# Another order for the sixteen-tile round of an attention kernel: scores and keys-as-rows in runs of two pairs, value products in runs of two

## The chip, the cores and the metric

The kernel runs on one core of a Trainium2 chip. The metric is the device time of one execution in microseconds. Engines are called as in the profile: PE is TensorE (matmuls; PEld its weight loads), DVE VectorE, ACT ScalarE, POOL GpSimd, SP SyncE, which issues the DMAs.

## The reference

Four sequences (B = 4) of 2048 rows of 256 numbers go through two layers, each with a residual and a layer norm.

```python
# first layer: 16 heads of 16; the value row is weighed with the sum of the row's softmax over m
att = softmax(einsum('blhd,bmhd->blmh', q, k) * scale, axis=2)
opt = einsum('blmh,blhd->blhd', att, v)
x = layernorm(x + opt @ w_out.T + b_out)
# second layer: the 4 best of 16 heads of 64 are chosen for each sequence, then attention
idx = sort(top_k(softmax(mean(x @ Wr + br, axis=1)), 4))
score = softmax(einsum('bhqd,bhkd->bhqk', Qs, Ks) * scale, axis=-1)
x = layernorm(x + (score @ Vs) @ Wo + bo)
```

All inputs and outputs are float32.

## The kernel before

A program on the host, `plan()`, writes out the order of the work of each engine before the kernel is built, and the kernel issues its instructions in these orders. For PE it keeps seven lists of units, each in order of due times, which `work_lists()` makes. Whenever PE is free in the planner's own small model of time, it takes the unit with the earliest due time among the heads of the lists whose inputs are ready and for which banks of PSUM are free. A unit that can't start yet is passed over for one of another list.

The units that matter here, with their lines:

- **A**, a tile of the first layer: two matmuls (L987) give 128 x 1024 scores of one head in two banks, DVE takes the negated row maximum (`nmax`, L1320), ACT the exponential with its sum (L1131, an ACTIVATE and a read of the accumulator). The banks are free when ACT is done. A batch has 16 heads x 16 row tiles x 2 halves = 512 tiles.
- **S**, a score of the second layer: four matmuls (L1052) for two heads at once, in the two halves of the array's rows, into two banks. DVE reduces them to maxima (`smax`, L1386), which frees the banks.
- **T**, the keys-as-rows form of the same product: four matmuls (L1067) and two small ones that subtract the maximum (L1070), in two banks. ACT takes the exponential into one of six slots of `probs` (L1246), which frees the banks.
- **V**, a value product: four matmuls (L1087) in the two halves of the array's columns. Four steps accumulate in one bank, from the first to ACT's copy of it (L1256). V of a step needs the exponentials of all four steps.
- POOL sums the exponentials (L896). Once in 16 steps a group ends: M (L1058) turns the maxima to rows, D (L1102) sums over partitions, R (L1110) spreads the reciprocals, and FQ, FO, FK, FV (L960, L945) are projections.

PSUM has eight banks; A, S and T take two each. While batch b is in its second layer, the tiles of batch b + 1 run between its steps. This is laid down in rounds of four steps (`BURST = 4`): a string gives the due times of a round's units by their place in it. A round takes S of steps ahead and T and V of steps one group (16 steps) behind. `ROUNDS[16]` has 16 tiles, `ROUNDS[12]` has 12, `ROUNDS[0]` (last batch) none, and `LEAD` opens the first and the last batch. Which is used:

```python
        if r < behind or b == B - 1 and k < behind:
            spots = LEAD
        elif b + 1 < B:
            spots = ROUNDS[16 if A_TILES - given[b] > 12 * (rounds - k) - EARLY else 12]
        else:
            spots = ROUNDS[0]
```

with 32 rounds in a batch, `behind` = 4, `given` the tiles already given out (32 at a batch's start, `AHEAD`), and `EARLY` = 8.

Of the kernel before, what the change touches and what calls it, by code (L numbers as in the profile page):

```python
# [42 lines left out]
BURSTS = STEPS // BURST  # L43
AHEAD = 32
EARLY = 8
ROUNDS = {0: "TSSTSTSTVVVV", 12: "AASTAASTSATASTAAAVVAAVAV", 16: "STAASTAASTAASTAAAVAVAAVAAVAA"}
LEAD = "SAAAASAAAASAAAASAAAATTTTVVVV"


# [28 lines left out]
def work_lists():  # L78
# [37 lines left out]
    for r in range(B * rounds + behind):  # L116
# [3 lines left out]
# [4 lines that stand above are left out]
        take = {"S": r * BURST, "T": r * BURST - STEPS, "V": r * BURST - STEPS}  # L124
# [1334 lines left out]
```

## Time and profile before

| | us |
|---|---|
| median of three runs | 3801.54 |
| lowest and highest | 3799.16, 4034.18 |
| the profiled execution | 3804.1 |
| its span, first to last instruction | 3802.2 |
| PE busy | 3517.9 |
| DVE busy | 3359.8 |
| ACT busy | 3063.9 |
| POOL busy | 1795.5 |

Busy times are of the whole span. Matmuls overlap in PE's pipeline, so a busy PE is not a PE at its peak. Idle time of an engine counts only where the others wait for it. The mean granted clock of TensorE is 0.953 of full speed (2.4 GHz).

### The profile page before, as it was taken

Reading aid. Unit: us, or ns where it says so; the run is one execution under the profiler, and the core shown is the slowest. Engines: PE = TensorE matmul, PEld = TensorE weight load, DVE = VectorE, ACT = ScalarE, POOL = GpSimd, SP = SyncE. Lnnn points to the kernel's source line nnn. Section 1 sums busy time; section 2 is a strip of 40 time slices with the busy share of each in tenths; the row PEclk is TensorE's granted clock in tenths of the full one; section 3 lists DMA queues with packets and bytes.
Section 4 is the critical chain, followed back from the end, with each engine's and each line's share of the span. In section 5 each row is a group of like instructions: output and inputs, shape, how many; then the busy total and the mean of one; then the engine's idle time right before and its main releaser. Section 6 shows DMA issues by size and latency. Waiting matters only on the chain.

```text
span 3802.2 us, 42635 instructions
## 1 busy us (share of the span) xinstructions
PE 3517.9 (93%) x14196; PEld 1270.9 (33%) x14196; DVE 3359.8 (88%) x3347; ACT 3063.9 (81%) x5097; POOL 1795.5 (47%) x1296
## 2 busy tenths in 40 slices
PE   8999989889999999899999999899999999899998
PEld 4323323332232323333232323433232323343333
DVE  7999999989999999889999999889999998567776
ACT  6999999879989998788999898788999998423333
POOL 6134433404443545445344445544444445657776
PEclk9988888889999999999999999899999999899999
DMA  6122222200010101200010101200010100100000
GB/s 201 50 81 81 86 76 66 85 17 17 17 28 17 28 17 37 77 13 24 17 28 17 28 17 31 82 9 29 17 28 17 28 17 17 49 1 12 12 12 12
DMA packets 117198, 142.67 MB, mean 38 GB/s; under 512 B 33395, under 2 KB 100467, under 8 KB 116979
## 3 DMA queue, kind: packets, MB, share of 16 engines
q1 hardware_dynamic: 116978, 139.95, 12.5%
q8 instruction: 114, 1.87, 0.2%
q14 instruction: 106, 0.86, 0.1%
HBM read 89.55 MB, written 50.33 MB: 37 GB/s over the span
## 4 chain that ended last, share of the span: by engine, by line
PE 44%; DVE 31%; ACT 17%; issue 4%; POOL 2%; SPq 1%; DMA 0%; DVEq 0%; POOLq 0%; ACTq 0%
DVE nmax L1320 21%; ACT ps L1131 15%; PE ps L1087 10%; PE ps L987 9%; PE ps L1052 7%; DVE smax L1386 7%; PE ps L1067 6%; PE ps L960 5%; PE ps L945 3%; PE ps L1102 1%; PE ps L1070 1%; DVE y L786 1%; DVE st L1298 1%; POOL y L786 1%; DVE y L1295 1%
## 5 line engine op out<-in xcount | busy, mean ns | idle before, releaser
L1320 DVE TENSOR_REDUCE nmax<-ps 128x1 f32<-128x1024 f32 x2048 | 2383.7, 1215 | 154.8 <-PE ps L987 146.3
L1131 ACT ACTIVATE ps<-ps,nmax 128x1024 f32<-128x1024 f32 x2048 | 2236.3, 1109 | 274.3 <-DVE nmax L1320 245.9
L987 PE MATMUL ps<-stack 96*128 96x512 bf16 x4524 | 1341.1, 402 | 174.2 <-ACT ps L1131 90.5
L896 POOL TENSOR_TENSOR facc<-facc,probs 128x1024 f32<-128x1024 f32 x443 | 1043.6, 2356 | 680.3 <-ACT probs L1246 603.1
L987 PEld LDWEIGHTS ps<-stack 96*128 96x128 bf16 x4524 | 326.7, 100 | 1314.0 <-ACT ps L1131 806.9
L1386 DVE TENSOR_REDUCE smax<-ps 128x2 f32<-128x1024 f32 x512 | 620.0, 1217 | 129.0 <-PE ps L1052 128.3
L1052 PE MATMUL ps<-fk,fq 64*128 64x512 f32 x2048 | 576.3, 645 | 29.6 <-ACT ps L1131 27.6
L1067 PE MATMUL ps<-fq,fk 64*128 64x512 f32 x2048 | 549.2, 615 | 5.3 <-DVE probs L1416 2.6
L1087 PE MATMUL ps<-probs,vals 128*64 128x512 f32 x2048 | 519.6, 614 | 5.4 <-DVE oT L1434 3.6
L1131 ACT ACTIVATION_READ_ACCUMULATOR ps<-ps,nmax 128x1 f32 x2048 | 451.9, 221 | 0.0
L1246 ACT ACTIVATE probs<-ps 128x1024 f32<-128x1024 f32 x384 | 391.5, 1020 | 70.1 <-PE ps L1070 69.8
L1235 ACT ACTIVATE probs<-probs 128x1024 f32<-128x1024 f32 x128 | 135.2, 1056 | 206.9 <-DVE probs L1416 146.0
L1067 PEld LDWEIGHTS ps<-fq,fk 64*128 64x128 f32 x2048 | 188.2, 189 | 266.1 <-issue 126.8
L1052 PEld LDWEIGHTS ps<-fk,fq 64*128 64x128 f32 x2048 | 165.3, 188 | 273.4 <-ACT ps L1131 156.4
L902 POOL TENSOR_TENSOR oacc<-oacc,part 128x512 f32<-128x512 f32 x72 | 90.9, 1263 | 275.8 <-ACT part L1256 275.8
L1087 PEld LDWEIGHTS ps<-probs,vals 128*64 128x64 f32 x2048 | 117.2, 136 | 277.6 <-issue 213.6
L762 POOL CAST fk<-vals 128x512 bf16<-128x512 f32 x60 | 36.6, 610 | 355.9 <-DVE vals L1326 331.9
L893 POOL TENSOR_TENSOR facc<-probs 128x1024 f32<-128x1024 f32 x32 | 75.3, 2355 | 262.5 <-ACT probs L1246 228.9
L1416 DVE TENSOR_TENSOR probs<-ps,stack 128x1024 f32<-128x1024 f32 x128 | 154.7, 1216 | 42.9 <-PE ps L1067 23.5
L1070 PE MATMUL ps<-frows,minus 64*128 64x512 bf16 x768 | 150.0, 383 | 0.0
L960 PE MATMUL ps<-fq,w_inT 128*128 128x512 f32 x256 | 141.4, 674 | 1.1 <-DVE qk_bias L1279 0.3
L960 PE MATMUL ps<-x1T,wqk_sel 128*128 128x512 f32 x256 | 133.8, 621 | 4.4 <-DMA bqk_sel<-in_L_ffn_bq 4.2
(134 smaller groups left out, 2021.0 us busy)
## 6 DMA issues: line engine op xcount, KB each, us to landing
stack<-qk_levels SPq DMA_DIRECT2D x768, 64.0 KB, 2.2
qk_levels<-fk SPq DMA_DIRECT2D x64, 384.0 KB, 2.5
probs<-in_L_attn_x SPq DMA_DIRECT2D x16, 512.0 KB, 3.9
v_rows<-vals SPq DMA_DIRECT2D x16, 512.0 KB, 2.7
vrows<-v_rows SPq DMA_DIRECT2D x16, 512.0 KB, 3.4
res<-in_L_attn_x SPq DMA_DIRECT2D x16, 512.0 KB, 4.0
x_rows<-y SPq DMA_DIRECT2D x16, 512.0 KB, 2.9
res<-x_rows SPq DMA_DIRECT2D x16, 512.0 KB, 3.9
```

What stands on the lines that cost most here:

```text
L896: pool.tensor_tensor(total, total, probs[:, slot, :], ALU.add).then_inc(facc_ready, 1)
L960: last = pe.matmul(bank(banks[0]), wT(cc), columns(cc), start=(cc == 0), stop=(cc == KC - 1))
L987: last = pe.matmul(bank(banks[i]), stack[0:SK, hd % 2, 0, t * P:(t + 1) * P], stack[0:SK, hd % 2, 1, col:col + CH], start=True, stop=True)
L1052: last = pe.matmul(bank(banks[h]), fq[rows, pair, qs:qs + P], fk[rows, pair, ks:ks + CH], start=True, stop=True)
L1067: last = pe.matmul(bank(banks[h]), fk[rows, pair, s * P:(s + 1) * P], fq[rows, pair, c * CH:(c + 1) * CH], start=True, stop=b + 1 == B)
L1070: last = pe.matmul(bank(banks[h]), minus16[rows, :], frows[rows, g % 2, :], start=False, stop=True)
L1087: last = pe.matmul(ps[rows, into, :], vals[:, s, (2 * pair + h) * FD:(2 * pair + h + 1) * FD], probs[:, slot_of(b, g, s), h * CH:(h + 1) * ...
L1131: act.activation(src, src, ACT.Exp, bias=nmax[:, b % 2, half, t, hd:hd + 1], scale=-1.0, accum_out=esum[:, b % 2, half, t, hd:hd + 1]).the ...
L1246: act.activation(probs[:, slot_of(b, g, s), :].rearrange("p (h n) -> p h n", h=2), two_banks(banks), ACT.Exp, scale=float(FD) ** -0.5).the ...
L1320: dve.tensor_reduce(nmax[:, b % 2, half, t, hd:hd + 1], two_banks(banks), AX.XY, ALU.min).then_inc(min_ready, 1)
L1386: dve.tensor_reduce(smax[:, g % 2, s // NCH, :, s % NCH], two_banks(banks), AX.X, ALU.max).then_inc(smax_ready, 1)
L1416: dve.tensor_tensor(probs[:, slot_of(b, g, s), :].rearrange("p (h n) -> p h n", h=2), two_banks(banks), bc[:, g % 2, :].rearrange("p (h n) ...
```

## The change

One string of due times gets another order. It has the same 28 units: four S, four T, four V and sixteen A. Before, each pair S T had two tiles behind it (three behind the last), and V came singly with one or two tiles between. After, two pairs S T S T run together, then four tiles, again two pairs and four tiles, then two V, four tiles, two V, four tiles.

```diff
@@ -43,7 +43,7 @@
 BURSTS = STEPS // BURST
 AHEAD = 32
 EARLY = 8
-ROUNDS = {0: "TSSTSTSTVVVV", 12: "AASTAASTSATASTAAAVVAAVAV", 16: "STAASTAASTAASTAAAVAVAAVAAVAA"}
+ROUNDS = {0: "TSSTSTSTVVVV", 12: "AASTAASTSATASTAAAVVAAVAV", 16: "STSTAAAASTSTAAAAVVAAAAVVAAAA"}
 LEAD = "SAAAASAAAASAAAASAAAATTTTVVVV"
```

No instruction is added or taken away. The orders of all engines, and the banks that the units get, come out of the planner anew.

## Rows read from the trace of the kernel before

**Rows 1.** The page, busy time and share of the span by engine.

```profile
PE 3517.9 (93%) x14196; PEld 1270.9 (33%) x14196; DVE 3359.8 (88%) x3347; ACT 3063.9 (81%) x5097; POOL 1795.5 (47%) x1296
```

**Rows 2.** Groups by line from 1700 to 2200 us: shapes, count, busy, mean, idle before.

```profile
L1386 DVE TENSOR_REDUCE smax<-ps 128x2 f32<-128x1024 f32 x80 | 97.3, 1216 | 4.7 <-PE ps L1052 4.7
```

**Rows 3.** Waits of DVE from 1700 to 2200 us: total us, times, longest.

```profile
DVE nmax L1320 <- PE ps L987: 20.1, 55, 1.5
DVE smax L1386 <- PE ps L1052: 4.7, 10, 0.9
```

**Rows 4.** DVE's timeline of one round: start, us, instruction, idle before and its cause.

```profile
1964.18 1.22 DVE L1386 TENSOR_REDUCE smax<-ps 128x2 f32<-128x1024 f32 x1
...
1975.57 3.48 DVE L1320 TENSOR_REDUCE nmax<-ps 128x1 f32<-128x1024 f32 x3
1979.23 1.22 DVE L1320 TENSOR_REDUCE nmax<-ps 128x1 f32<-128x1024 f32 x1 [0.20 <-PE ps L987]
1980.78 6.88 DVE L1320 TENSOR_REDUCE nmax<-ps 128x1 f32<-128x1024 f32 x6 [0.32 <-PE ps L987]
1987.58 1.21 DVE L1386 TENSOR_REDUCE smax<-ps 128x2 f32<-128x1024 f32 x1
```

**Rows 5.** Windows of 10 us: length, busy PE, PEld, DVE, ACT, POOL, clock, DMA.

```profile
1680.00:1690.00 10.00, 10.00 (x47) 4.42 (x47) 8.45 (x8) 8.68 (x15) 5.71 (x3) 1.00 0.01 2
...
1810.00:1820.00 10.00, 10.00 (x34) 3.67 (x34) 6.58 (x8) 7.00 (x13) 0.61 (x1) 0.67 0.31 81
```

**Rows 6.** PE's timeline of the same round.

```profile
1965.35 0.60 PE L987 MATMUL ps<-stack 96*128 96x512 bf16 x2 [0.31 <-ACT probs L1246]
1965.88 1.13 PE L1052 MATMUL ps<-fk,fq 64*128 64x512 f32 x4
1966.84 1.02 PE L1067 MATMUL ps<-fq,fk 64*128 64x512 f32 x4
...
1968.02 0.60 PE L987 MATMUL ps<-stack 96*128 96x512 bf16 x2
...
1976.72 1.94 PE L1087 MATMUL ps<-probs,vals 128*64 128x512 f32 x8
1978.59 0.60 PE L987 MATMUL ps<-stack 96*128 96x512 bf16 x2
1979.13 1.08 PE L1087 MATMUL ps<-probs,vals 128*64 128x512 f32 x4
1980.14 1.04 PE L987 MATMUL ps<-stack 96*128 96x512 bf16 x4
1981.11 1.08 PE L1087 MATMUL ps<-probs,vals 128*64 128x512 f32 x4
...
1983.30 1.17 PE L987 MATMUL ps<-stack 96*128 96x512 bf16 x4 [0.58 <-ACT ps L1131]
...
1985.98 1.13 PE L1052 MATMUL ps<-fk,fq 64*128 64x512 f32 x4 [0.49 <-ACT ps L1131]
```

**Rows 7.** PE's timeline elsewhere, S and T without tiles between.

```profile
1507.01 1.02 PE L1067 MATMUL ps<-fq,fk 64*128 64x512 f32 x4
...
1508.08 1.02 PE L1052 MATMUL ps<-fk,fq 64*128 64x512 f32 x4
1508.94 1.02 PE L1067 MATMUL ps<-fq,fk 64*128 64x512 f32 x4
```

**Rows 8.** ACT's timeline, the exponential that follows 1980.78 on DVE.

```profile
1982.04 1.09 ACT L1131 ACTIVATE ps<-ps,nmax 128x1024 f32<-128x1024 f32 x1 [0.34 <-DVE nmax L1320]
```

**Rows 9.** PE's timeline in batch 0, the first and last of five single tiles.

```profile
562.31 0.60 PE L987 MATMUL ps<-stack 96*128 96x512 bf16 x2
...
566.51 0.60 PE L987 MATMUL ps<-stack 96*128 96x512 bf16 x2 [0.49 <-ACT ps L1131]
```

**Rows 10.** Windows of 1 us there, columns as in the windows above.

```profile
567.00:568.00 1.00, 0.51 (x2) 0.13 (x2) 1.00 (x2) 1.00 (x3) 0.00 (x0) 0.70 0.00 0
568.00:569.00 1.00, 0.94 (x3) 0.13 (x2) 1.00 (x2) 1.00 (x3) 0.00 (x0) 0.50 0.42 127
```

## The prediction

> **What bounds the kernel now.** I read the page's busy times first: PE stands at 93% and DVE at 88% of the span [rows 1], so either could be the bound, and the average doesn't decide it. So I went to the stretch that the change touches. The sixteen-tile round is used 74 times: batch 0 enters its fifth round with 96 of 512 tiles given out, and the rule in the code then picks it 22 times; batches 1 and 2 begin with 32 given and pick it 26 times each. From 1700 to 2200 us (inside batch 1) there are 80 score reductions [rows 2], four to a round, so 20 rounds in 500 us: **25 us a round**. One microsecond a round is 74 us, 1.95% of the time; about 2% is also what a measurement of this kernel can tell from no change.
>
> In that stretch DVE waits for PE for 20.1 us ahead of tile minima and 4.7 us ahead of score maxima [rows 3], 1.24 us a round. That is all that any new order can win from DVE: 92 us over the 74 rounds.
>
> Then one undisturbed round in the timeline. On DVE [rows 4] it runs from the score at 1964.18 to the score at 1987.58, 23.4 us for 20 reductions. Six in a row begin at 1980.78 and the next at 1987.58, so one takes 1.13 us from start to start and 20 take 22.7. The 0.7 us left over are two gaps in the part with value products: three reductions begin at 1975.57, so the fourth could begin at 1978.96 but begins at 1979.23 (0.27 late); the next could begin at 1980.36 and begins at 1980.78 (0.42). In the part with scores and keys-as-rows DVE has no gap. There PE is the one that waits, and for banks. So in most rounds **the loop DVE, ACT, free bank, PE is the bound, with DVE full**, and PE's own time is cover. Some rounds are otherwise: at 1680 to 1690 us PE is busy all of the time and DVE 8.45 of 10 [rows 5]; the two batches' first four rounds carry late projections and look like this, 8 rounds in all.
>
> **The change, part by part.**
>
> *Fewer turns on PE.* From a tile to a score PE needs 0.53 us (1965.35 to 1965.88), score to keys-as-rows 0.96, keys-as-rows to the next tile 1.18 (1966.84 to 1968.02) [rows 6]. A tile ahead of another tile costs 0.43: a tile, a tile and the turn to a value product take 0.97 (1980.14 to 1981.11), and one tile with that turn 0.54 (1978.59 to 1979.13) [rows 6]. In a run without tiles, keys-as-rows to score takes 1.07 and score to keys-as-rows 0.86 [rows 7]. Two separate pairs are 2 x (0.53 + 0.96 + 1.18) = 5.34 us; two in a run, with the second tile's turn now a plain tile, 0.53 + 0.96 + 1.07 + 0.86 + 1.18 + 0.43 = 5.03. That is 0.3 saved, twice a round: 0.6. A single value product takes 1.01 and its turn 0.54, two together 1.87 [rows 6]. Two singles are 2 x 1.55 = 3.10, two together 0.54 + 1.87 + 0.43 = 2.84. The planner already runs the first two together, so only the last two can gain: 0 to 0.26. PE saves 0.6 to 0.86 us a round. Where PE waits for a bank this is worth nothing; I count 0.6 in the 8 rounds in which PE is full: -5 us.
>
> The trace shows this price of a turn at about 0.1 us each way. The Trainium skill, TensorEngine Tiling (Array Packing), Key Properties, says that a change of tiling mode drains TensorE; by that rule alone the new order, with half of the turns, is a gain. The rows agree that a turn costs something, but also that PE isn't late in most rounds.
>
> *DVE runs dry behind each run of two pairs.* This is the main term. Tiles, scores and keys-as-rows need two of the eight PSUM banks each, so four are out at once. Behind four tiles, the four fills of the run take the pairs that these tiles give back, in order. Put the start of the fourth tile's reduction at 0. ACT starts its exponential 1.26 us later (1980.78 to 1982.04), and PE can start the next fill on the freed banks 1.26 us after that (1982.04 to 1983.30) [rows 4, 6, 8]: 2.52. That fill is the second keys-as-rows; 1.18 later PE starts the first new tile, and DVE can begin it 0.64 after PE (1980.14 to 1980.78) [rows 4, 6]: 4.34. Meanwhile DVE has only the two scores, and is through at 3 x 1.13 = 3.39. **DVE stands still for 0.95 us.** If the second keys-as-rows takes the first score's banks instead, it can start at 1.13 + 1.22 and what a read bank takes to reach PE, at most 0.17 (1.26 less the exponential's 1.09) and by my estimate 0.05: 2.40, and the gap is 0.83. I take 0.87, nearer to that, since the score ends first; twice a round: 1.74. In the old order two tiles come between any two pairs and this gap doesn't arise [rows 4]. PE's saving doesn't shorten the chain, since 1.18 of it is the turn that stays.
>
> *The value products.* The fourth tile takes the pair that the last keys-as-rows frees, at the moment at which the first product becomes ready, so that one must wait for the first tile's banks: 2.52 on a clock that starts with the first tile's reduction. Two products take 1.87: 4.39; the fifth tile reaches DVE 0.64 later, 5.03, where DVE was through at 4 x 1.13 = 4.52. Gap 0.51. The last two I expect one at a time in PE's waits for banks, for the planner gives PE anything that can start; they cost DVE nothing. So 0.51 against 0.69 before: -0.18.
>
> *Sum of a round:* 1.74 - 0.18 = +1.56 us. 66 rounds: +103. From this up to 0.55 us a round may come back (the stretch's 1.24 less the plain round's 0.69, 36 us in all), where projections and the like now fall into a tail with spare PE time; I take a third, -12. Other engines: POOL gets its four sums a round in two pairs and has room between; SP's queue and the DMAs keep their order, and the maximum row's chain starts two places earlier. I count nothing for these; without that cover, a late sum on POOL (2.36 us) would hold one exponential a round, unlikely as each slot is reused six steps later.
>
> *The clock.* Behind the last product, PE has some five tiles, one for each 1.13 us of DVE, until the next score. In batch 0 such single tiles ran from 562.31 to 566.51 us, five of them with 0.3 to 0.5 us idle before four [rows 9], and between 567 and 568 us the granted clock fell from 1.0 to 0.5 of full speed, 2.4 to 1.2 GHz [rows 10]. In batch 1 the same fall covers most of 1810 to 1820 us: mean clock 0.67, DVE busy 6.58 of 10 [rows 5], against 9.7 in the plain round (0.7 us of gaps in 23.4): **3.1 us lost**. There it follows the 128-row sums of a group. The old tail of single tiles (from 1982.12, where the last product ends, to 1985.98 [rows 6], 3.9 us) kept its clock; the new one is 5 us or so. I expect the fall in nine more rounds, about half of the rounds with a group's sums: +28. Ends: none (0) and all of the 74 (+229).
>
> Total: -5 + 103 - 12 + 28 = **+114 us**. The profiled execution took 3804.1 us (span 3802.2); the median of the runs is 3801.5, the same within 0.1%. Forecast: 3804 + 114 = **3918 us**.
>
> **The rivals.**
>
> *PE is the bound after all.* For: 93% busy, and PE full in rows of some rounds. Then 0.6 to 0.86 us a round are won, 44 to 63 us: about **3750**. This ends on the other side, not slower. It decides if DVE's gap behind a run stays under 0.3 us, that is if more fills are out than I count. Against: in the plain round PE's starts wait for ACT and DVE [rows 6], and DVE has no gap where pairs and tiles alternate [rows 4].
>
> *The order in the string isn't the order that runs.* The string is only due times; the planner takes the earliest unit whose inputs and banks are there. Already now it turns V A V A A V into V V A V A A V. If a tile slips in front of the second keys-as-rows, or a bank pair is free early, the gap shrinks to that of the value part and the sum to 0 +- 25: about **3800**. Against: a tile needs the same two banks, and is due later.
>
> *The clock falls in most rounds.* Three rounds in four at 3.1 us: +174, with the +86 of the rest (-5 + 103 - 12): about **4060**. For: [rows 9, 10]. Against: in batch 0 nothing but tiles ran, while here a dense run and four products precede, and the 3.9 us tail holds its clock.
>
> The Trainium skill, TensorE: Matmul & The Clock Gate, HAM oscillation, describes such a re-throttling between bursts; the row at 567 us shows it for this kernel, and whether the longer tail brings it, no row here shows.
>
> **How the numbers follow.** Forecast 0.50 (3870 to 3965); order not kept or gap hidden 0.20 (3785 to 3830); PE bound 0.10 (3735 to 3765); clock falling in most rounds 0.20 (3990 to 4120). Leaving out the PE case and the upper half of the clock case leaves out 2 in 10: 3785 to 4030. Slower by over 2% begins at 3878: nearly nine tenths of the forecast and all of the clock case, less some for a gap smaller than worked out, 0.57; faster by over 2% needs more than PE can save in this sum, 0.05; the rest, 0.38, within 2%.
>
> **What would show it.** DVE's waits for PE between 1700 and 2200 us should rise from 1.24 to about 2.7 us a round, with a repeated gap of 0.6 to 1 us ahead of the first tile minimum behind each run; a round should take 26.5 us instead of 25; keys-as-rows to score should read 1.07 and score to keys-as-rows 0.86 inside a run; more stretches at half clock in tails. I am wrong if DVE has no gap behind the second keys-as-rows, if the order on PE isn't S T S T A A A A, or if rounds without a fall of the clock take 24 us as before.

## The result and the profile after

The changed kernel takes 3907.18 us (median of four, 3906.13 to 3907.79) against 3800.35 us in the same session: **2.8% slower**, ratio 1.0284, 95% interval 1.0264 to 1.0305. The ratio leaves out one disturbed execution of the kernel before (4034.18 us). The profiled execution has a span of 3904.9 us, 102.7 more than before, and a mean granted clock of 0.950 against 0.953.

Where the time went is read first from windows that cut the span where the kind of round changes. Columns are the length of the window and the busy time of PE, PEld, DVE, ACT and POOL, then clock and DMA. The kernel before, its three stretches of sixteen-tile rounds with a twelve-tile stretch between:

```profile
860.00:1408.00 548.00, 510.08 (x2114) 158.67 (x2114) 518.37 (x477) 505.71 (x832) 235.92 (x143) 0.98 0.08 20
1408.00:1612.00 204.00, 180.82 (x790) 74.91 (x788) 182.81 (x217) 162.57 (x286) 111.31 (x99) 0.95 0.19 54
1612.00:2266.00 654.00, 615.56 (x2566) 205.32 (x2564) 603.26 (x558) 590.89 (x972) 293.73 (x180) 0.98 0.08 21
...
2472.00:3118.00 646.00, 608.11 (x2570) 201.90 (x2568) 603.42 (x559) 591.45 (x974) 293.71 (x180) 0.99 0.08 21
```

The changed kernel, cut at the same units of work:

```profile
859.00:1438.00 579.00, 499.68 (x2110) 164.30 (x2110) 521.68 (x476) 503.06 (x830) 235.49 (x143) 0.97 0.06 19
1438.00:1643.00 205.00, 184.78 (x790) 78.05 (x788) 182.15 (x217) 163.04 (x286) 111.22 (x99) 0.93 0.18 54
1643.00:2328.00 685.00, 603.06 (x2567) 211.86 (x2564) 609.03 (x558) 589.93 (x972) 293.26 (x180) 0.98 0.07 20
...
2535.00:3220.00 685.00, 602.98 (x2569) 211.20 (x2566) 609.60 (x559) 590.73 (x974) 293.27 (x180) 0.98 0.07 20
```

The three stretches grew by 31, 31 and 39 us, 101 of the 102.7; the twelve-tile stretch didn't move. That is 1.37 us for each of the 74 rounds. In them DVE did the same work in more time (603 us busy of 654, then 609 of 685), and PE was less busy than before, not more (616 us, then 603).

DVE's waits from 1700 to 2200 us (total, times, longest), which answer to [rows 3]:

```profile
DVE nmax L1320 <- PE ps L987: 28.0, 62, 0.9
DVE smax L1386 <- PE ps L1052: 20.2, 40, 1.8
```

The same stretch has 74 score reductions now, 18.5 rounds: 48.2 / 18.5 = 2.6 us a round, where it was 1.24. The waits of scores have grown most, from 4.7 to 20.2 us.

DVE's timeline of one round, beside [rows 4]:

```profile
2009.52 1.22 DVE L1386 TENSOR_REDUCE smax<-ps 128x2 f32<-128x1024 f32 x1
2010.93 1.23 DVE L1386 TENSOR_REDUCE smax<-ps 128x2 f32<-128x1024 f32 x1 [0.20 <-PE ps L1052]
2012.71 4.62 DVE L1320 TENSOR_REDUCE nmax<-ps 128x1 f32<-128x1024 f32 x4 [0.54 <-PE ps L987]
2017.24 1.22 DVE L1386 TENSOR_REDUCE smax<-ps 128x2 f32<-128x1024 f32 x1
2018.66 1.23 DVE L1386 TENSOR_REDUCE smax<-ps 128x2 f32<-128x1024 f32 x1 [0.20 <-PE ps L1052]
2020.43 4.62 DVE L1320 TENSOR_REDUCE nmax<-ps 128x1 f32<-128x1024 f32 x4 [0.54 <-PE ps L987]
2025.46 9.28 DVE L1320 TENSOR_REDUCE nmax<-ps 128x1 f32<-128x1024 f32 x8 [0.41 <-PE ps L987]
```

At 1.13 us from start to start, the second score of a run comes 0.28 us late, the tile behind it 0.65, both runs alike, and the fifth tile of the value part 0.51. That is 2.37 us of gaps a round against 0.69. Four tiles fit exactly between 2012.71 and 2017.24, so DVE has no gap among them.

PE in the second of these runs, beside [rows 6, 7]:

```profile
2016.35 1.13 PE L1067 MATMUL ps<-fq,fk 64*128 64x512 f32 x4
2017.32 0.38 PE L1070 MATMUL ps<-frows,minus 64*128 64x512 bf16 x2
2017.53 1.08 PE L1052 MATMUL ps<-fk,fq 64*128 64x512 f32 x4
2018.51 1.13 PE L1067 MATMUL ps<-fq,fk 64*128 64x512 f32 x4
2019.47 0.38 PE L1070 MATMUL ps<-frows,minus 64*128 64x512 bf16 x2
2019.79 1.90 PE L987 MATMUL ps<-stack 96*128 96x512 bf16 x8
2022.95 1.94 PE L1087 MATMUL ps<-probs,vals 128*64 128x512 f32 x8 [1.26 <-ACT ps L1131]
```

The first score starts on DVE at 2017.24, the second keys-as-rows on PE 1.27 us later, the first new tile 1.28 us after that, and DVE has it at 2020.43, 0.64 later: 3.19 us, in which DVE has two reductions (2.26). The gap is 0.93. Which banks the second keys-as-rows waits for is in the list of those who waited for score reductions (total us, times). In the three stretches of the changed kernel, 859 to 1438, 1643 to 2328 and 2535 to 3220 us:

```profile
PEld ps L1067: 20.7, 32
PEld ps L1067: 23.4, 39
PEld ps L1067: 24.2, 40
```

These are 111 waits for 148 runs (two in each of 74 rounds), where the kernel before has none, 3 and 3: in three runs of four the second keys-as-rows waits for the banks of the run's first score. For the other 37 the list names no such wait.

### The profile page after: what moved, and what is told of

Its sections match the earlier page's. It is cut to its first block, busy times and chain, and to the rows that moved or that the text cites. A ratio compares the mean times of both kernels' runs of the same rounds, so it can differ in the third digit from the quotient of the medians.

```text
span 3904.9 us, 42630 instructions
## 1 busy us (share of the span) xinstructions
PE 3492.8 (89%) x14196; PEld 1294.4 (33%) x14196; DVE 3377.4 (86%) x3347; ACT 3060.2 (78%) x5097; POOL 1793.6 (46%) x1296
## 4 chain that ended last, share of the span: by engine, by line
PE 51%; ACT 25%; DVE 16%; issue 5%; POOL 2%; SPq 1%; DMA 0%; DVEq 0%; POOLq 0%; ACTq 0%
ACT ps L1131 22%; PE ps L1052 12%; PE ps L1067 12%; DVE nmax L1320 11%; PE ps L1087 9%; PE ps L987 8%; PE ps L960 5%; PE ps L945 2%; PE ps L1070 2%; DVE smax L1386 1%; DVE st L1298 1%; DVE y L786 1%; ACT part L1256 1%; POOL y L786 1%; DVE y L1295 1%
## 5 line engine op out<-in xcount | busy, mean ns | idle before, releaser
L987 PE MATMUL ps<-stack 96*128 96x512 bf16 x4524 | 1284.2, 401 | 125.9 <-ACT ps L1131 92.6
L987 PEld LDWEIGHTS ps<-stack 96*128 96x128 bf16 x4524 | 352.1, 100 | 1147.2 <-ACT ps L1131 718.4
L1067 PE MATMUL ps<-fq,fk 64*128 64x512 f32 x2048 | 575.5, 641 | 14.8 <-ACT ps L1131 10.1
L1067 PEld LDWEIGHTS ps<-fq,fk 64*128 64x128 f32 x2048 | 178.8, 192 | 335.1 <-ACT ps L1131 125.5
```

Source lines behind the costliest of these rows:

```text
L987: last = pe.matmul(bank(banks[i]), stack[0:SK, hd % 2, 0, t * P:(t + 1) * P], stack[0:SK, hd % 2, 1, col:col + CH], start=True, stop=True)
L1067: last = pe.matmul(bank(banks[h]), fk[rows, pair, s * P:(s + 1) * P], fq[rows, pair, c * CH:(c + 1) * CH], start=True, stop=b + 1 == B)
```

## The experiments

Each is compared with the kernel before in the same session. The line that is changed in the diffs is that of the kernel before, unless said otherwise; of the line `ROUNDS`, only the entry 16 is shown.

Executions of one kernel differ a little in their mean clock, and in time with it. The kernel before ran 40 times beside the experiments: at a mean clock of 0.950 it took 3813 and 3816 us, at 0.958 from 3784 to 3791, and a straight line through all 40 falls by 2.9 us for each 0.001, with a spread of 2 us around it. Small differences are therefore also compared with this line at the same mean clock (an estimate; the clock is given to 0.001). By it the changed kernel is 97 us slower, so some 10 of its 107 us go with its lower clock.

**Only the value products moved.**

```diff
-16: "STAASTAASTAASTAAAVAVAAVAAVAA"
+16: "STAASTAASTAASTAAVVAAAAVVAAAA"
```

> Only the value products move: the pairs stay as before (S T A A four times, with two tiles and not three behind the last), the tail is V V A A A A V V A A A A. Theory (DVE runs dry behind a run of two pairs, because the banks come back one by one): no run of pairs, so no gap; the time stays at 3800, 0 +- 15 us. Rival 1 (the value products in twos hold PE for 1.87 us each and take the time): +50 us or more, about 3850. Rival 2 (the planner puts them where PE has room, whatever the string says): the same 3800, and the order on PE in the value part is almost that of before.

Measured: 3807.43 us, ratio 1.0006 (0.9985 to 1.0028): no change. DVE's waits from 1700 to 2200 us:

```profile
DVE nmax L1320 <- PE ps L987: 18.9, 54, 1.5
DVE smax L1386 <- PE ps L1052: 4.6, 10, 0.8
```

They are those of before. PE's order in the value part is still V V A V A A V in this kernel, as rival 2 had it: the string gives due times, and a value product after the first two goes out when no tile can. Moving the value products by itself costs nothing; the loss of the changed kernel comes with its runs of pairs.

**A tile between the two pairs of a run.**

```diff
-16: "STAASTAASTAASTAAAVAVAAVAAVAA"
+16: "STASTAAASTASTAAAVVAAAAVVAAAA"
```

> One tile is put between the two pairs of each run (S T A S T A A A, twice), the tail as in the changed kernel. Theory, worked from the rows of after: the second score now waits for the last tile's banks (2.52 us behind that tile's reduction), DVE gets it at 3.65 instead of 3.39, the next tile at 5.30 instead of 4.78: 0.26 + 0.52 = 0.78 us a run against 0.93 measured in the changed kernel, so 20 to 35 us less than after: 3870 to 3890. Still clearly slower than before, since the fourth fill behind four tiles is on the chain as before. Rival (only the back-to-back turn of the run costs, so a tile between the pairs heals it): near 3800.

Measured: 3850.09 us, ratio 1.0129 (1.0112 to 1.0146). Half of the loss stays, and 57 us come back against the changed kernel, not 20 to 35. DVE's timeline of this kernel:

```profile
1970.22 1.22 DVE L1386 TENSOR_REDUCE smax<-ps 128x2 f32<-128x1024 f32 x1
1971.35 1.22 DVE L1320 TENSOR_REDUCE nmax<-ps 128x1 f32<-128x1024 f32 x1
1972.67 1.23 DVE L1386 TENSOR_REDUCE smax<-ps 128x2 f32<-128x1024 f32 x1
1974.27 4.62 DVE L1320 TENSOR_REDUCE nmax<-ps 128x1 f32<-128x1024 f32 x4 [0.37 <-PE ps L987]
1979.08 8.01 DVE L1320 TENSOR_REDUCE nmax<-ps 128x1 f32<-128x1024 f32 x7 [0.20 <-PE ps L987]
```

The second score is 0.19 late and the tile behind it 0.47: 0.66 a run. I had 0.78. What I left out is the value part: with three tiles and not four behind a run, the first two value products don't wait for a tile's banks (in the changed kernel they stood 1.26 us), and the fifth tile is 0.29 late, not 0.51. Two runs at 0.27 less and 0.22 in the value part make 0.76 a round, 56 us in 74. A tile between heals only part, as the chain has it.

**All four pairs in one run.**

```diff
-16: "STAASTAASTAASTAAAVAVAAVAAVAA"
+16: "STSTSTSTAAAAAAAAVVAAAAVVAAAA"
```

> All four pairs of a round in one run, S T S T S T S T, then eight tiles, then the tail of the changed kernel. PE makes the fewest turns of all. Theory: behind the second pair PE itself is too slow for DVE (1.93 us a pair against 1.13 us a reduction): gaps of 0.29, 0.92, 0.80 and 0.51 us, 2.5 us in one run a round, against 2 x 0.93 = 1.86: +0.66 us in 74 rounds, about 49 us above after, 3940 to 3970. Rival (what counts is PE's turns, and the loss of the changed kernel comes from elsewhere): below after, 3907 or less. Rival (each run costs about the same, whatever its length): half of the loss, about 3855.

Measured: 4068.11 us, ratio 1.0705 (1.0687 to 1.0723). Right in sign and far off in size: 161 us above the changed kernel, where 49 were expected. The mean granted clock was 0.908. Windows of 2 us in this kernel's row of eight tiles show what was left out of that sum:

```profile
2006.00:2008.00 2.00, 0.74 (x5) 0.11 (x2) 2.00 (x3) 1.53 (x3) 1.92 (x3) 1.00 0.00 0
2008.00:2010.00 2.00, 1.38 (x5) 0.14 (x3) 2.00 (x3) 2.00 (x5) 1.86 (x2) 0.63 0.00 0
2010.00:2012.00 2.00, 1.90 (x4) 0.25 (x4) 2.00 (x2) 2.00 (x3) 1.23 (x1) 0.50 0.00 0
2012.00:2014.00 2.00, 1.91 (x5) 0.53 (x6) 2.00 (x3) 2.00 (x5) 0.00 (x0) 0.50 0.00 0
2014.00:2016.00 2.00, 2.00 (x8) 0.45 (x5) 0.35 (x1) 1.59 (x4) 0.00 (x0) 0.66 0.00 0
```

PE has one tile for each of DVE's reductions and is busy 0.74 of 2 us; the granted clock then falls to 0.5, 1.2 GHz. The two value products behind the row start at that clock, and DVE gets 0.35 of 2 us of work.

**The same with the later tiles of a long row computed twice.** The kernel has a rule that repeats a tile's matmuls when work is queued for DVE and no score, keys-as-rows or value product was among PE's last `NEAR` units. On top of the edit above:

```diff
-NEAR = 12
+NEAR = 4
```

> The run of four pairs again (4068 us), now with the tiles from the fifth of a long row on computed twice on PE (the kernel's own rule for this, NEAR, from 12 units to 4; the order of the work is the same). In the run before, the granted clock fell in the row of eight single tiles (2008 to 2015 us) and again later, and its mean was 0.908. Theory: of its 161 us above the changed kernel, some 50 are the gaps behind the pairs, and the rest, 110, is the fallen clock; with PE kept busy in the long rows the clock stays up: mean about 0.95, 3950 to 3990. Rival (the gaps alone make the loss, or the second matmuls cost as much as they save): 4040 to 4080.

Measured: 3951.87 us, ratio 1.0416 (1.0386 to 1.0446); 116 us came back. Its clock and its DVE timeline:

```profile
core 0: 3949.6 us, clock 0.950
```

```profile
2006.94 1.21 DVE L1386 TENSOR_REDUCE smax<-ps 128x2 f32<-128x1024 f32 x1
2008.56 1.23 DVE L1386 TENSOR_REDUCE smax<-ps 128x2 f32<-128x1024 f32 x1 [0.41 <-PE ps L1052]
2010.49 1.23 DVE L1386 TENSOR_REDUCE smax<-ps 128x2 f32<-128x1024 f32 x1 [0.71 <-PE ps L1052]
2012.42 1.23 DVE L1386 TENSOR_REDUCE smax<-ps 128x2 f32<-128x1024 f32 x1 [0.71 <-PE ps L1052]
2014.03 9.14 DVE L1320 TENSOR_REDUCE nmax<-ps 128x1 f32<-128x1024 f32 x8 [0.38 <-PE ps L987]
```

The gaps of the run are 0.49, 0.80, 0.80 and 0.48, 2.57 us against 2 x 0.93 in the changed kernel: 0.71 x 74 = 53 us, and the kernel is 45 us above the changed one, at the same mean clock. So of the 161 us, some 45 were gaps and 116 came with the clock. The split is rough, for the rule also repeats tiles outside the rows of eight.

**Keys-as-rows without its subtraction,** in the changed kernel and in the one before, with orders and banks as they were. The two small matmuls are left out, so the exponentials are of scores from which no maximum is taken:

```diff
-                                             fq[rows, pair, c * CH:(c + 1) * CH], start=True, stop=b + 1 == B)
-                        for h, rows in two if b + 1 < B else []:
-                            last = pe.matmul(bank(banks[h]), minus16[rows, :], frows[rows, g % 2, :],
-                                             start=False, stop=True)
+                                             fq[rows, pair, c * CH:(c + 1) * CH], start=True, stop=True)
```

> The changed kernel without the two small matmuls that subtract the maximum from keys-as-rows (L1070): the exponentials are then of the scores as they are; all orders, banks and waits stay. A keys-as-rows unit keeps PE 0.31 us less. Theory: the second one of a run stands on the chain from DVE's last score to the first new tile, so every run's gap gets 0.31 us shorter: 2 x 0.31 x 74 = 46 us, and beside it what the kernel before also gains (see the other run). 3907 - 46 - 15 to 35 = 3825 to 3845. Rival (PE's busy time is what counts, wherever it stands): the same gain in both kernels, 4 x 0.31 x 74 = 92 us or none. Rival (the gap behind a run comes from ACT taking two exponentials in a row): no change beyond what the kernel before gains, about 3880.

> The kernel before, without the same two small matmuls (exponentials of the scores as they are; orders, banks and waits as before). Theory: in most sixteen-tile rounds PE's time is cover, so only the rounds in which PE is full gain: 8 rounds with late projections, 18 twelve-tile rounds and the first four, at most 4 x 0.31 us each, 37 us in all; I expect 15 to 35, 3765 to 3785. Rival (PE is the bound throughout): 92 us and more, about 3705.

Measured: the changed kernel 3856.76 us, ratio 1.0148 (1.0133 to 1.0163), 50 us less than with the subtraction; the kernel before 3768.29 us, ratio 0.9919 (0.9903 to 0.9935), 32 us less. The second lies in its range, and far from the 92 of a PE that is the bound throughout. The first misses its 3825 to 3845. DVE in the changed kernel without the subtraction (its lines are three earlier):

```profile
1990.07 1.22 DVE L1383 TENSOR_REDUCE smax<-ps 128x2 f32<-128x1024 f32 x1
1991.49 1.23 DVE L1383 TENSOR_REDUCE smax<-ps 128x2 f32<-128x1024 f32 x1 [0.20 <-PE ps L1052]
1993.04 4.62 DVE L1317 TENSOR_REDUCE nmax<-ps 128x1 f32<-128x1024 f32 x4 [0.33 <-PE ps L987]
```

The second score's gap stays at 0.29 and the tile's falls from 0.65 to 0.42: the chain got shorter by 0.22, not by 0.31. The 0.31 held a turn: the two small matmuls take 0.21 when a score follows (2017.32 to 2017.53 in the changed kernel) and 0.32 when a tile does (2019.47 to 2019.79), and the 0.1 of the turn stays when they go. Two runs a round at 0.22 are 33 us; by the same price the 92 are 62.

The kernel before gained in another place than expected. In the profiled executions its three stretches of sixteen-tile rounds are 33 us shorter, of 39 that the span lost, and the two twelve-tile stretches only 3. In the three stretches it has 29 us at half clock, where it had 64 with the subtraction, so about half of the 33 can be the clock. The rest says that PE's time for keys-as-rows isn't all cover in sixteen-tile rounds either.

By the ratios the changed kernel gained 20 us more than the other, give or take 11 by the three intervals. At the same mean clock it gained 47 (from 97 to 50) and the other 26, so 21 more: the clock doesn't hide the rest of the 33, and where that went stays open. What is shown is that the gap behind a run moves with the length of the keys-as-rows unit, as a link of the chain must, and that ACT's two exponentials in a row are not what holds it.

**The changed kernel with later tiles of a row computed twice.** In the changed kernel:

```diff
-NEAR = 12
+NEAR = 3
```

> The changed kernel, its order unchanged, with every tile from the fourth of a row on computed twice on PE (NEAR from 12 to 3). This asks how much of the changed kernel's loss is the clock falling in tails of single tiles. My prediction counted nine more falls, 28 us. The traces say otherwise: the granted clock's mean is 0.950 after and 0.953 before, nearly the same. Theory (the loss is gaps of DVE, the clock falls as often as before): 3907, less the falls in plain tails that are now kept up, 0 to 30 us; DVE's gap of 0.9 us behind each run stays. Rival (the clock's falls are the loss): 3830 or less.

Measured: 3880.51 us, ratio 1.0212 (1.0198 to 1.0226), mean clock 0.961. Falls of the clock in rows of tiles of the changed kernel are worth 27 us; the other 81 us of its loss stay. At the same mean clock it is 99 us above the kernel before, where the changed kernel was 97: the second matmuls gave back clock and left the gaps. The same edit in the kernel before was not measured.

**No runs at all.**

```diff
-16: "STAASTAASTAASTAAAVAVAAVAAVAA"
+16: "AAASATASATAASTAASTAAAVAAAVVV"
```

> An order with no run of pairs at all, and for half of the scores a tile between the score and its keys-as-rows too: A A A S A T A S A T A A S T A A S T A A A V A A A V V V. Theory: DVE's queue never holds less than a tile behind a keys-as-rows, so the gaps ahead of tile minima shrink by 0.1 to 0.2 us a round: 5 to 15 us below before, at best 0.4%, 3785 to 3800. The rest of DVE's waits in a round (0.69 us) stand in the value part, which the planner orders alike for all strings. Rival (more turns of PE, 0.2 us each, cost more): 10 to 30 us above before.

Measured: 3787.71 us, ratio 0.9968 (0.9956 to 0.9980): **0.3% faster than the kernel before**. Its waits of DVE from 1700 to 2200 us:

```profile
DVE nmax L1320 <- PE ps L987: 14.5, 52, 1.4
DVE smax L1386 <- PE ps L1052: 4.3, 4, 2.2
```

18.8 us against 24.8 before. The string's value products stand last but run where they did. That the gain comes from shorter gaps, as expected, isn't shown: the mean clock was also higher (0.958 against 0.954, medians of the runs), and at the same clock 2 us of the 13 are left, no more than the spread. Whether this order keeps the clock up or these runs had it by chance stays open.

## Why the prediction was right, step by step

The forecast was 3918 us, 114 above the profiled execution of before; measured were 107 by the medians and 102.7 by the spans. That the total came so near is in part luck: without the clock +86 was forecast and some 97 measured, and for the clock +28 and some 10, two misses that nearly cancel.

- *DVE runs dry behind each run.* 0.87 us a run was forecast, 0.93 measured. In three runs of four the second keys-as-rows does take the first score's banks, the lower end of the bound (0.83), and in the round shown it starts 1.27 us behind that score's start as worked out; but to the next tile it needs 1.28 us and not 1.18: its four large matmuls take 0.96 (2018.51 to 2019.47), 0.1 more than in the kernel before (1966.84 to 1967.70). The last-tile chain of 0.95 came near by accident. Inside a run, keys-as-rows to score and score to keys-as-rows were to read 1.07 and 0.86; they read 1.18 and 0.98 (2016.35, 2017.53, 2018.51), and only the run of four pairs has the short times.
- *The value products.* Gap forecast 0.51, measured 0.51; the last two go out one at a time between tiles (1.54 us apart, a tile between), as expected, and the order of the string counts for nothing there (the first experiment).
- *A plain round* came to +1.68 us (2.37 - 0.69) against +1.56. Over 74 rounds 1.37 were measured: the rest came back in rounds that also hold projections. One of these, from score to score, took 26.91 us before (1937.27 to 1964.18) and 27.11 after (1982.41 to 2009.52). I had 8 such rounds at -0.6 and 12 us given back; the sum without the clock (+86) is 11 below the 97 us at the same mean clock.
- *The clock* was the term mis-sized: nine more falls at 3.1 us, +28 us. The share of the clock not granted, (1 - mean) x span, is 179 us before and 195 after, 16 more; a fall such as that of [rows 5] has 3.3 us of it and cost 3.1, so some 15 us; at the same mean clock it is some 10. The falls were more than forecast and shorter: in the three stretches the granted clock is at half in 12 places before, 64 us together, and in 26 after, 88 us. So there were 14 more and not nine, and 24 us more at half clock, half of which is 12. Doubling tiles gave 27 us back, but the kernel before has falls of its own.
- *PE's turns* were counted at next to nothing, and so they were. By the rule of the Trainium skill, TensorEngine Tiling (Array Packing), Key Properties, that a change of tiling mode drains TensorE, the order with the fewest turns should gain. Here the fewest turns (one run of four pairs) gave 4.2% more time even with the clock held up, and the order with the most gave 0.3% less. A turn does cost time (a pair in the run of four is 1.93 us on PE, alone with its turns 0.3 longer), but in most rounds PE wasn't late.

The rivals: PE as the bound is refuted by the gap of 0.93 us behind a run, which was to stay under 0.3, and by a slower kernel in which PE is less busy. The shorter keys-as-rows in the kernel before gave 32 us and not 92; against the 62 of the price measured, some of PE's time does count there. That the string isn't the order that runs holds for the value products and not for the pairs. The clock falling in most rounds didn't happen in the changed kernel (26 falls in 74 rounds), but did in the run of four pairs (88 falls), whose rows of eight tiles have nothing between. In [rows 9, 10], too, the clock fell while tiles ran, with at most 0.49 us idle between them. The Trainium skill, Perfetto Trace Analysis, Optimization Strategy, says that one gap repeated over a stretch on the engine that should be full can mean too little SBUF or PSUM for the next tile. The gap of DVE behind each run, with 111 waits in 148 runs for the first score's banks, is such a gap, and here it came from the order in which four pairs of banks are given back, at an unchanged number of banks.

## What to carry to other kernels

When several kinds of work share few buffers and one engine drains most of them, follow one buffer from its release to the next work for the full engine: release, fill of whatever comes first, fill of the next useful tile. If that is longer than the queue ahead of the engine (here 3.19 us from the first score's start, against two reductions of 1.13), it stands still each time, and here grouping like with like, which spares the filling engine its turns, made it worse. And look at what the filling engine does in the stretch that the grouping leaves bare: here a row of eight tiles cost more by its clock (116 us) than by its gaps (45). And compare small differences at the same mean clock before calling them an effect of the order.

## What the runs showed of the hardware

In the row of eight tiles the granted clock of TensorE fell to half (from 2.4 to 1.2 GHz) while PE still had a tile for each of DVE's reductions of 1.13 us and never stood idle for longer than 1.3 us: it was busy 0.74 of 2 us just before. Computing the same tiles twice, which is work thrown away, raised the mean clock from 0.908 to 0.950 in that kernel and from 0.951 to 0.961 in the changed one, and was worth 116 and 27 us. A second keys-as-rows of a run took 0.1 us more to the next tile than the one of [rows 6] (1.28 against 1.18). The two small matmuls at its end take 0.21 us ahead of a score and 0.32 ahead of a tile; leaving them out shortened the chain by 0.22.
